# Two rows of indirect sends regrouped into four, in an attention loop followed by a mixture of experts

## The chip, the cores and the metric

The kernel runs on one core of a Trainium2 chip. The metric is the device time of one execution in microseconds (us). Engines: PE is TensorE (PEld its weight loads), DVE is VectorE, ACT is ScalarE, POOL is GpSimd, SP is SyncE.

## The reference

One transformer block over 32 batches of 256 rows of 256 numbers: a two-way cross attention (8 heads of 64) and a layer of 16 experts, of which each row takes its best four.

```python
def _L0_xattn_ref(x, context, Wq1, ..., Wout, bout):
    # q1,k1,v1 from x; q2,k2,v2 from context; 8 heads of 64
    attn1 = jax.nn.softmax(einsum('bhid,bhjd->bhij', q2, k1) * SCALE, axis=-1)
    out1  = einsum('bhij,bhjd->bhid', attn1, v1)
    attn2 = jax.nn.softmax(einsum('bhid,bhjd->bhij', q1, k2) * SCALE, axis=-1)
    out2  = einsum('bhij,bhjd->bhid', attn2, v2)
    out = out1 * alpha + out2 * (1.0 - alpha)
    ...
    return out @ Wout + bout

def _L0_ffn_ref(hidden_states, gate_w, w1, w3, w2):
    probs = jax.nn.softmax(x @ gate_w.T, axis=-1)
    topk_w, topk_idx = jax.lax.top_k(probs, 4)
    topk_w = topk_w / jnp.sum(topk_w, axis=-1, keepdims=True)
    ...
    act = silu(x @ w1[e]) * (x @ w3[e])
    out = sum over the four experts of topk_w * (act @ w2[e])

x = x + _L0_xattn_ref(_layernorm(x), ctx_1024, ...)
x = x + _L0_ffn_ref(_layernorm(x), ...)
```

## The kernel before

The program is written by hand: every engine has its own list of instructions, and the engines meet in semaphores. It has two long stages. In the attention loop `stage_a` calls an engine's `iteration(b, nxt, cur, prev, old)` once for each batch b; b = 2 to 30 is a real loop on the chip, and b = -1, 0, 1, 31, 32 and 33 stand before and behind it. The work of a batch spreads over several iterations: `nxt` starts batch b+1, `cur` is most of batch b, `prev` ends the attention of batch b-1, and `old` ends the routing of batch b-2. After the loop `stage_b` runs 80 groups of 256 rows through the experts, and a last part adds the results up.

The attention of a batch has eight steps, u = 0 to 7, each for two heads. For a step PE computes the scores into the PSUM tile `p_s`, DVE takes the negative row maxima (`nmx`, line 856), ACT takes the exponential (`probs`, line 619), DVE the reciprocal of the sums (`inv`, line 863, semaphore `inv_set`), and POOL multiplies in four instructions of one half head each (`normalise`, line 521, semaphore `normed_p`). PE transposes each head's 256 columns (`probs_half`, line 1150, semaphore `pt_done`), once it sees `normed_p` for that head: two of the four instructions for head 0, four for head 1. ACT copies head 0's half out of the PSUM tile `p_pt` (`probsT`, line 607, semaphore `pt_out_a`), DVE head 1's (line 760, `pt_out_b`), and PE multiplies with the values (`attend`, line 1170). The step of interest is the last one, u = 7 of batch b-1, which is worked off in iteration b. Behind its transposes PE stands before `project(b, 9)`, a query projection that writes into the bank of `p_pt` that ACT's copy reads, and so waits for `pt_out_a` of step 7.

POOL also sends. `send(i)` (line 513) is an indirect DMA that scatters 128 rows of 260 numbers from the tile `routed` to the rows of `x_rows` in HBM that `slot_i` names: a batch has eight of them (two halves of its rows, four experts each). The sends of batch b-2 stand in iteration b, behind two waits: for the slots from DVE (`router_step`, line 848) and for ACT's copies of the rows (`copies_set`, line 708). `rows_sent` counts them. DVE waits for it in the same iteration, before it writes `routed` for batch b-1 (`norm_apply`, line 778), which in turn needs POOL's reciprocal root `rstd` (`rsqrt`, line 508). That chain begins with `x_mid` (DVE, line 922), the output projection plus `x_res`; POOL writes `x_res` for the next batch (line 541) once `x_mid` has been read.

The order on POOL is the order in which the code is written; nothing reorders it.

Of the kernel before, what the change touches and what calls it, by code (L numbers as in the profile page):

```python
# [16 lines left out]
TOP_K = 4  # L17
# [4 lines left out]
def wait_alone(eng, sem, count):  # L22

    eng.wait_ge(sem, count)
    eng.nop(nofuse=True)
# [8 lines left out]
def spread(ap, axis, shape):  # L34

    return ap.unsqueeze(axis).to_broadcast(shape)


def wait(eng, sem, count):

    if isinstance(count, int) and count <= 0:
        return
    eng.wait_ge(sem, count)


def xattn_moe_kernel(nc, x, ctx, Wq1, Wk1, Wv1, Wq2, Wk2, Wv2, alpha_attn, Wout, bout,
# [8 lines left out]
    ST = S // P  # L55
    PAIRS = INNER // P
    STEPS = 2 * PAIRS
# [27 lines left out]
    with ExitStack() as stack:  # L85
# [218 lines left out]
        def norm1(b):  # L304

            return 1 if isinstance(b, int) and b == 0 else 2 * b

        def norm2(b, cur):

            return 2 * b + 1 if cur else 2 * b  # L310
# [33 lines left out]
        def stage_a(eng, body):  # L344
            body(-1, True, False, False, False)
            body(0, True, True, False, False)
            body(1, True, True, True, False)
            with eng.Fori(2, B - 1) as b:
                body(b, True, True, True, True)
            body(B - 1, False, True, True, True)  # L350
            body(B, False, False, True, True)
            body(B + 1, False, False, False, True)
# [3 lines left out]
        def stage_b(eng, body, before=0, after=3):  # L356

            for j in range(-before, LOADS):
                body(j, j % LOADS)
            with eng.Fori(1, GROUPS // LOADS - 1) as q:  # L360
                for r in range(LOADS):
                    body(LOADS * q + r, r)
            for j in range(GROUPS - LOADS, GROUPS + after):
                body(j, j % LOADS)

        def exists(j):

            return not isinstance(j, int) or 0 <= j < GROUPS
# [112 lines left out]
        @block.gpsimd  # L481
        def _(pool):
            for t in (ident, before, ones, routed):
                v = t[tuple([slice(None)] * len(t.shape))]
                pool.memset(v, 1.0 if t is ones or t is before else 0.0).then_inc(consts_set, 1)
            pool.wait_ge(consts_set, 4)
            pool.affine_select(out=ident[:, :], in_=ident[:, :], compare_op=ALU.not_equal, fill=1.0,
                               base=0, pattern=[[-1, P]], channel_multiplier=1).then_inc(consts_set, 1)

            pool.affine_select(out=before[:, :], in_=before[:, :], compare_op=ALU.is_gt, fill=0.0,  # L490
                               base=0, pattern=[[1, P]], channel_multiplier=-1).then_inc(consts_set, 1)
            pool.iota(pad_target[:, :, :], [[GROUP, 2 * E], [P, 2]], base=DUMP, channel_multiplier=1).then_inc(consts_set, 1)
            pool.memset(mhalf[:, :], -0.5).then_inc(consts_set, 1)
            for t, pattern, start, mult in (
                    (expert[:, :], [[1, E]], 0, 0),
                    (region[:, :], [[REGION, E]], 0, 0),
                    (base[:, :], [[REGION, E]], 0, 0),
                    (target[:, :, :], [[P * TOP_K, ST], [1, TOP_K]], 0, TOP_K),
                    (fills[:, :], [[GROUP, MOST]], 0, 0),
                    (tri[:, :, :], [[1, E], [-1, E]], 0, 0),  # L500
                    (group_no[:, :], [[P, TC]], 0, 1)):
                pool.iota(t, pattern, base=start, channel_multiplier=mult,
                          allow_small_or_imprecise_dtypes=True).then_inc(consts_set, 1)
            pool.wait_ge(const_in, 16 * N_CONST)

            def rsqrt(n):
                pool.wait_ge(ve_set, n)
                pool.tensor_tensor(rstd[:, :], ve[:, :], mhalf[:, :], ALU.pow).then_inc(rstd_set, 1)

            def send(i):  # L510

                t, k = i // TOP_K, i % TOP_K
                pool.indirect_dma_start(x_rows, bass.IndirectOffsetOnAxis(ap=slot_i[:, t, k:k + 1], axis=0),  # L513
                                        routed[:, t, k, :], None).then_inc(rows_sent, 16)

            def normalise(b, u):
                pool.wait_ge(inv_set, STEPS * b + u + 1)
                pr, rc = probs[u % 2], inv[u % 2]
                for h, t in ((0, 0), (0, 1), (1, 0), (1, 1)):
                    g = 2 * h + t  # L520
                    pool.tensor_tensor(pr[:, h, t, :], pr[:, h, t, :], rc[:, g:g + 1].to_broadcast([P, S]),  # L521
                                       ALU.mult).then_inc(normed_p, 1)

            def iteration(b, nxt, cur, prev, old):
                if prev:
                    normalise(b - 1, STEPS - 1)
                if old:
                    wait_alone(pool, router_step, ROUTER_STEPS * (b - 1))
                    wait_alone(pool, copies_set, b - 1)
                    for i in range(6):  # L530
                        send(i)
                if cur:
                    normalise(b, 0)
                    normalise(b, 1)
                if old:
                    for i in range(6, ST * TOP_K):
                        send(i)
                if cur:
                    wait(pool, mid_set, b)
                    pool.wait_ge(x_landed, 16 * (b + 1))  # L540
                    pool.tensor_tensor(x_res[:, :, :], x_in[:, :, :], spread(bias[:, :], 1, [P, ST, D]),
                                       ALU.add).then_inc(x_res_set, 1)
                if prev:
                    rsqrt(norm2(b, cur))
                if cur:
                    normalise(b, 2)
                    normalise(b, 3)
                if nxt:
                    rsqrt(norm1(b + 1))
                if cur:  # L550
                    for u in range(4, STEPS - 1):
                        normalise(b, u)

            stage_a(pool, iteration)

            def return_group(j, r):

                if exists(j):
                    wait_alone(pool, y_set, j + 1)
                    for i in range(2):  # L560
                        pool.indirect_dma_start(  # L561
                            y_rows, bass.IndirectOffsetOnAxis(ap=xg[r][:, i, D:D + 1].bitcast(I32), axis=0),
                            y_out[r % 4][:, i, :], None).then_inc(y_sent[r % 4], 16)

            stage_b(pool, return_group, after=0)
# [832 lines left out]
```

## Time and profile before

| | us |
|---|---|
| median of 3 runs | 2364.32 |
| lowest and highest of them | 2360.82 and 2365.71 |
| the profiled execution | 2342.8 |
| its span | 2341.0 |
| PE busy in the span | 1951.1 (83%) |
| POOL busy in the span | 1215.2 (52%) |

The attention loop takes the first two thirds of the span. In it a batch's period is the time from one batch's first send to the next batch's. The page's chain of work that ended last walks back from the last instruction to whatever released each step; "another core or an unknown queue" there, and "remote" in an engine's rows, stand for a release by something that the profile doesn't name. A row of the timeline gives start, duration, engine, line, operation, output and inputs, and in brackets the engine's idle time before it with what ended that.

### The profile page before, as it was taken

How to read it: one execution, taken by the hardware profiler on the slowest of the kernel's cores; microseconds unless marked ns; L12 is line 12 of the kernel's file. 1: busy time of each engine (PE TensorE's matmuls, PEld its weight loads, DVE VectorE, ACT ScalarE, POOL GpSimd, SP SyncE). 2: the span in 40 equal slices, each digit the busy share in tenths (PEclk: the TensorE clock that was granted, in tenths of full speed). 3: DMA queues.
4: the chain of work that ended last, by engine and by line, in shares of the span. 5: the costliest groups of instructions: out<-in, count | busy, mean ns of one | idle time of the engine just before them, and what ended most of it. 6: DMA issues, size and time to landing. Idle time of an engine off the chain costs nothing.

```text
span 2341.0 us, 52570 instructions
## 1 busy us (share of the span) xinstructions
PE 1951.1 (83%) x15778; PEld 1681.2 (72%) x15779; DVE 1423.4 (61%) x3205; ACT 1240.9 (53%) x3605; POOL 1215.2 (52%) x1683
## 2 busy tenths in 40 slices
PE   5799989999999998999999999995488888888700
PEld 4688877888777887788877878784377777777600
DVE  3466666666666676666666666665454444444488
ACT  4666656666566665666656666663144444444400
POOL 2356556656556565665655655564254545455500
PEclk9999999999999999999999999997699999999955
DMA  3511011110101101111011110114775444444399
GB/s 115 151 45 37 32 45 36 41 36 32 44 33 45 36 32 45 36 41 36 32 43 34 45 36 32 36 39 131 168 206 171 141 137 137 139 137 143 120 390 365
DMA packets 158599, 210.56 MB, mean 90 GB/s; under 512 B 24273, under 2 KB 131425, under 8 KB 158562
## 3 DMA queue, kind: packets, MB, share of 16 engines
q1 hardware_dynamic: 119394, 127.75, 18.2%
q0 software_dynamic: 26112, 71.86, 8.7%
q10 hardware_dynamic: 13056, 10.50, 1.6%
q8 instruction: 18, 0.29, 0.1%
q14 instruction: 19, 0.16, 0.0%
HBM read 113.02 MB, written 97.03 MB: 90 GB/s over the span
## 4 chain that ended last, share of the span: by engine, by line
PE 68%; another core or an unknown queue 11%; DVE 7%; ACT 4%; DMA 4%; issue 3%; SPq 2%; POOL 2%; ACTq 0%; POOLq 0%; DVEq 0%
PE p_av L1170 10%; PE p_pt L1150 9%; PE p_s L1074 7%; PE p_gu L1345 6%; PE p_s L1133 6%; PE p_y L1363 4%; PE p_x L1074 4%; PE p_s L1084 3%; DVE z_ahead L1044 3%; PE p_x L1203 3%; PE p_pt L1074 2%; PE p_xt L1334 2%; PE p_av L1074 2%; PE p_av L1084 2%
## 5 line engine op out<-in xcount | busy, mean ns | idle before, releaser
L521 POOL TENSOR_TENSOR probs<-probs,inv 128x256 f32<-128x256 f32 x1024 | 596.3, 615 | 496.0 <-DVE inv L863 495.9
L619 ACT ACTIVATE probs<-p_s,nmx 128x256 f32<-128x256 f32 x1024 | 474.0, 484 | 58.9 <-PE p_pt L1150 42.7
L856 DVE TENSOR_REDUCE nmx<-p_s 128x4 f32<-128x1024 f32 x256 | 312.4, 1221 | 254.2 <-PE p_s L1133 206.5
L561 POOL DMA_INDIRECT y_rows<-y_out,xg x288 | 276.3, 959 | 301.3 <-ACT y_out L731 231.1
L513 POOL DMA_INDIRECT x_rows<-routed,slot_i x256 | 253.8, 991 | 138.9 <-DVE target L848 69.1
L1150 PE MATMUL p_pt<-ident,probs 128*128 128x128 f32 x2048 | 293.8, 279 | 7.7 <-POOL probs L521 3.7
L607 ACT COPY probsT<-p_pt 128x512 f32<-128x512 f32 x256 | 151.4, 592 | 277.6 <-remote 152.7
L1170 PE MATMUL p_av<-probsT,val 128*64 128x256 f32 x2048 | 269.1, 408 | 2.0 <-ACT val L591 1.6
L1150 PEld LDWEIGHTS p_pt<-ident,probs 128*128 128x128 f32 x2048 | 227.7, 141 | 48.0 <-issue 17.8
L619 ACT ACTIVATION_READ_ACCUMULATOR probs<-p_s,nmx 128x1 f32 x1024 | 219.9, 215 | 0.0
L1170 PEld LDWEIGHTS p_av<-probsT,val 128*64 128x64 f32 x2048 | 144.3, 146 | 83.9 <-issue 28.0
L760 DVE COPY probsT<-p_pt 128x512 f32<-128x512 f32 x256 | 175.9, 687 | 45.3 <-PE p_pt L1150 33.6
L1015 DVE SCALAR_TENSOR_TENSOR gated<-gated,p_gu 128x256 f32<-128x256 f32 x144 | 60.0, 417 | 214.7 <-ACT gated L721 203.4
L1345 PE MATMUL p_gu<-wgu_hi,xgT_hi 128*128 x576 | 178.8, 310 | 11.4 <-issue 9.2
L721 ACT ACTIVATE gated<-p_gu 128x256 f32<-128x256 f32 x144 | 57.8, 402 | 239.9 <-PE p_gu L1345 139.3
L1133 PE MATMUL p_s<-kT_hi,qT_hi 64*128 64x256 f32 x1024 | 158.8, 306 | 9.6 <-ACT probs L619 7.5
L1345 PE MATMUL p_gu<-wgu_hi,xgT_lo 128*128 x576 | 165.1, 287 | 0.0
L1345 PE MATMUL p_gu<-wgu_lo,xgT_hi 128*128 x576 | 164.4, 285 | 0.0
L1074 PE MATMUL p_s<-rowsT_hi,wp_hi 128*128 128x256 f32 x512 | 151.8, 296 | 0.0
L1030 DVE TENSOR_TENSOR xgT_lo<-p_xt,xgT_hi 128x512 fp32r<-128x512 f32 x144 | 99.6, 692 | 76.7 <-ACT xgT_hi L736 54.9
L1133 PE MATMUL p_s<-kT_lo,qT_hi 64*128 64x256 f32 x1024 | 145.1, 280 | 0.4 <-issue 0.4
L1133 PE MATMUL p_s<-kT_hi,qT_lo 64*128 64x256 f32 x1024 | 144.7, 279 | 0.0
(192 smaller groups left out, 5199.3 us busy)
## 6 DMA issues: line engine op xcount, KB each, us to landing
xg<-x_rows SPq DMA_DIRECT2D x144, 257.0 KB
y_in<-y_rows SPq DMA_DIRECT2D x32, 1024.0 KB, 8.3
rows<-in_ctx_dram SPq DMA_DIRECT2D x32, 256.0 KB, 2.7
x_in<-in_x_dram SPq DMA_DIRECT2D x32, 256.0 KB, 2.7
mid_rows<-x_mid SPq DMA_DIRECT2D x32, 256.0 KB
z_ahead<-mid_rows SPq DMA_DIRECT2D x24, 256.0 KB
out_dram<-z_ahead ACTq DMA_DIRECT2D x24, 256.0 KB, 8.5
y_rows<-y_out,xg POOLq DMA_INDIRECT x288
```

What stands on the lines that cost most here:

```text
L513: pool.indirect_dma_start(x_rows, bass.IndirectOffsetOnAxis(ap=slot_i[:, t, k:k + 1], axis=0), routed[:, t, k, :], None).then_inc(rows_sen ...
L521: pool.tensor_tensor(pr[:, h, t, :], pr[:, h, t, :], rc[:, g:g + 1].to_broadcast([P, S]), ALU.mult).then_inc(normed_p, 1)
L561: pool.indirect_dma_start(y_rows, bass.IndirectOffsetOnAxis(ap=xg[r][:, i, D:D + 1].bitcast(I32), axis=0), y_out[r % 4][:, i, :], None).th ...
L607: act.copy(flat(probsT[u % 2][:, 0, :, :]), p_pt[:, 0, :]).then_inc(pt_out_a, 1)
L619: act.activation(probs[u % 2][:, h, t, :], p_s[:, 2 * (u % 2) + h, t * S:(t + 1) * S], ACT.Exp, bias=nmx[u % 2][:, g:g + 1], accum_out=sum ...
L760: dve.tensor_copy(flat(probsT[u % 2][:, 1, :, :]), p_pt[:, 1, :]).then_inc(pt_out_b, 1)
L856: dve.tensor_reduce(nmx[i][:, :], p_s[:, 2 * i:2 * i + 2, :].rearrange("p h (t k) -> p (h t) k", t=ST), AX.X, ALU.max, negate=True).then_i ...
L1074: mm = pe.matmul(proj_bank(n)[:, j * S:(j + 1) * S], wp[a][:, w, k, c:c + P], rowsT[w // 3][r][:, k, :], start=(i == 0), stop=(i == 5))
L1133: mm = pe.matmul(p_s[:, 2 * d + h, t * S:(t + 1) * S], qT[d][q][r:r + HEAD_DIM, p, t * P:(t + 1) * P], kT[d][k][r:r + HEAD_DIM, p, :], sta ...
L1150: mm = pe.transpose(p_pt[:, h, k * S + t * P:k * S + (t + 1) * P], probs[u % 2][:, h, t, k * P:(k + 1) * P], ident[:, :])
L1170: mm = pe.matmul(p_av[r:r + HEAD_DIM, 0:S], val[d][:, k, c:c + HEAD_DIM], probsT[u % 2][:, h, k, :], start=(d == 0 and k == 0), stop=(d == ...
L1345: mm = pe.matmul(p_gu[:, i, n, :], xgT[i][h][:, n, k, :], wgu[a][:, bass.ds(experts[r], 1), k, :, :].rearrange("p e g i -> p (e g i)"), st ...
```

## The change

POOL's iteration alone is rewritten. A batch's eight sends stood in two rows, six and two. Now they stand in rows of two, three and two, and one by itself: the first two between the halves of `normalise(b - 1, 7)` (head 0 before them, head 1 behind), then three, then as before the normalisations of steps 0 and 1, then two, then `x_res`, then the last one, ahead of `rsqrt`.

```diff
-            def normalise(b, u):
+            def normalise(b, u, heads=(0, 1)):
                 pool.wait_ge(inv_set, STEPS * b + u + 1)
                 pr, rc = probs[u % 2], inv[u % 2]
-                for h, t in ((0, 0), (0, 1), (1, 0), (1, 1)):
+                for h, t in [(h, t) for h in heads for t in range(ST)]:
...
                 if prev:
-                    normalise(b - 1, STEPS - 1)
+                    normalise(b - 1, STEPS - 1, (0,))
                 if old:
                     wait_alone(pool, router_step, ROUTER_STEPS * (b - 1))
                     wait_alone(pool, copies_set, b - 1)
-                    for i in range(6):
+                    for i in range(2):
+                        send(i)
+                if prev:
+                    normalise(b - 1, STEPS - 1, (1,))
+                if old:
+                    for i in range(2, 5):
                         send(i)
                 if cur:
                     normalise(b, 0)
                     normalise(b, 1)
                 if old:
-                    for i in range(6, ST * TOP_K):
+                    for i in range(5, 7):
                         send(i)
                 if cur:
                     wait(pool, mid_set, b)
                     pool.wait_ge(x_landed, 16 * (b + 1))
                     pool.tensor_tensor(x_res[:, :, :], x_in[:, :, :], spread(bias[:, :], 1, [P, ST, D]),
                                        ALU.add).then_inc(x_res_set, 1)
+                if old:
+                    send(7)
                 if prev:
                     rsqrt(norm2(b, cur))
```

On POOL, at the head of the loop's body (b = 2 to 30), where step 7 of batch b-1 is normalised and the sends of batch b-2 begin; L521 is `normalise`, L513 a send:

```order
-L521 TENSOR_TENSOR probs<-probs,inv 128x256 x4
+L521 TENSOR_TENSOR probs<-probs,inv 128x256 x2
 L24 REGISTER_ALU
-L513 DMA x_rows<-routed,slot_i 139264x260 x6
+L513 DMA x_rows<-routed,slot_i 139264x260 x2
+L521 TENSOR_TENSOR probs<-probs,inv 128x256 x2
+L513 DMA x_rows<-routed,slot_i 139264x260 x3
 L517 ISA
```

Head 1 of step 7 has moved behind the wait for the slots and behind two sends, and the row of six is now two, a pause of two normalisations, and three.

On POOL, further down in the same body, behind the normalisations of steps 0 and 1; L541 (L546 in the changed kernel) is `x_res`, L508 `rsqrt`:

```order
 L513 DMA x_rows<-routed,slot_i 139264x260 x2
-L540 ISA
-L541 TENSOR_TENSOR x_res<-x_in,bias 128x512
+L545 ISA
+L546 TENSOR_TENSOR x_res<-x_in,bias 128x512
+L513 DMA x_rows<-routed,slot_i 139264x260
 L507 ISA
 L508 TENSOR_TENSOR rstd<-ve,mhalf 128x2
```

The last send now stands between `x_res` and the `rstd` for which DVE waits. The other engines' lists are the same in both kernels.

## Rows read from the trace of the kernel before

**Rows 1.** The page: the chain of work that ended last, share of the span by engine

```profile
PE 68%; another core or an unknown queue 11%; DVE 7%; ACT 4%; DMA 4%; issue 3%; SPq 2%; POOL 2%; ACTq 0%; POOLq 0%; DVEq 0%
```

**Rows 2.** Timeline of PE, one batch (columns: start us, us, instruction)

```profile
736.71 0.66 PE L1150 MATMUL p_pt<-ident,probs 128*128 128x128 f32 x4
...
738.65 0.65 PE L1150 MATMUL p_pt<-ident,probs 128*128 128x128 f32 x4
742.25 0.38 PE L1074 MATMUL p_pt<-rowsT_hi,wp_hi 128*128 128x256 f32 x1 [2.95 <-ACT probsT L607]
...
744.03 3.40 PE L1170 MATMUL p_av<-probsT,val 128*64 128x256 f32 x16
```

**Rows 3.** Timeline of ACT, the same batch

```profile
741.62 0.59 ACT L607 COPY probsT<-p_pt 128x512 f32<-128x512 f32 x1 [5.56 <-remote]
```

**Rows 4.** All copies of line 607 in the span: why ACT waited, who waited

```profile
  remote: 152.7, 28
...
  PE p_pt L1074: 77.2, 26
```

**Rows 5.** Timeline of POOL, the same batch

```profile
733.07 1.06 POOL L513 DMA_INDIRECT x_rows<-routed,slot_i  x1 [1.81 <-DVE target L848]
...
739.50 0.96 POOL L513 DMA_INDIRECT x_rows<-routed,slot_i  x1 [0.30 <-issue]
...
750.41 0.96 POOL L513 DMA_INDIRECT x_rows<-routed,slot_i  x1 [0.30 <-issue]
753.51 1.29 POOL L541 TENSOR_TENSOR x_res<-x_in,bias 128x512 f32<-128x512 f32 x1 [2.13 <-DVE x_mid L922]
754.90 0.72 POOL L508 TENSOR_TENSOR rstd<-ve,mhalf 128x2 f32<-128x2 f32 x1
755.61 4.71 POOL L521 TENSOR_TENSOR probs<-probs,inv 128x256 f32<-128x256 f32 x8
```

**Rows 6.** Windows: busy time of PE, PEld, DVE, ACT, POOL, then PE's clock, DMA

```profile
742.25:749.00 6.75, 6.75 (x53) 4.75 (x53) 1.21 (x4) 4.46 (x18) 4.61 (x8) 0.75 0.00 0
```

**Rows 7.** Timeline of POOL: first sends of five batches, and one pause

```profile
190.75 1.06 POOL L513 DMA_INDIRECT x_rows<-routed,slot_i  x1 [1.81 <-DVE target L848]
...
831.88 1.06 POOL L513 DMA_INDIRECT x_rows<-routed,slot_i  x1 [1.81 <-DVE target L848]
836.24 0.97 POOL L513 DMA_INDIRECT x_rows<-routed,slot_i  x1 [3.30 <-issue]
...
877.86 1.06 POOL L513 DMA_INDIRECT x_rows<-routed,slot_i  x1 [1.81 <-DVE target L848]
...
1516.32 1.06 POOL L513 DMA_INDIRECT x_rows<-routed,slot_i  x1 [1.81 <-DVE target L848]
```

**Rows 8.** Timeline of ACT and of PE in the batch that begins at 831.88

```profile
836.21 0.59 ACT L607 COPY probsT<-p_pt 128x512 f32<-128x512 f32 x1 [1.35 <-PE p_pt L1150]
...
843.51 0.37 ACT L611 COPY attnT<-p_av 128x256 f32<-128x256 f32 x1 [2.57 <-remote]
```

```profile
843.36 0.40 PE L1133 MATMUL p_s<-kT_lo,qT_hi 64*128 64x256 f32 x2 [0.43 <-issue]
```

**Rows 9.** Timeline of DVE, then of PE, behind the sends

```profile
755.73 1.25 DVE L778 TENSOR_SCALAR routed<-x_mid,mv,rstd 128x256 f32<-128x256 f32 x2 [0.91 <-POOL rstd L508]
756.91 0.68 DVE L760 COPY probsT<-p_pt 128x512 f32<-128x512 f32 x1
```

```profile
759.40 1.95 PE L1170 MATMUL p_av<-probsT,val 128*64 128x256 f32 x16
```

**Rows 10.** DMA from 748 to 754 us in 40 slices (tenths busy)

```profile
DMA  0000000000000000047910000099500000000000
```

**Rows 11.** Timelines behind the loop (b = 32): ACT, POOL's last send, DVE

```profile
1613.85 0.37 ACT L611 COPY attnT<-p_av 128x256 f32<-128x256 f32 x1 [3.11 <-PE p_av L1170]
```

```profile
1617.95 0.96 POOL L513 DMA_INDIRECT x_rows<-routed,slot_i  x1 [0.30 <-issue]
```

```profile
1622.42 0.73 DVE L778 TENSOR_SCALAR routed<-x_mid,mv,rstd 128x256 f32<-128x256 f32 x2 [3.54 <-DMA x_rows<-routed,slot_i]
```

## The prediction

> **What bounds the kernel now.** I read the chain of work first: PE carries 68% of it, and the second largest share, 11%, is put down to nothing that the profile names [rows 1]. So the attention loop is bound by PE except where something unnamed holds it. The timelines of one batch show where. PE transposes head 0 of step 7 at 736.71, which takes 0.66, so ACT's copy could start at about 737.4. It starts at 741.62, after 5.56 idle that "remote" ended [rows 2, 3]: 4.2 us late. PE, done with head 1 at 739.30, stands still for 2.95 until that copy is out. All its other work in the loop runs back to back. The stall also costs clock: of the 6.75 us behind it, PE was granted 0.75 on average, that is 1.2 instead of 2.4 GHz for half of it, and the 16 matmuls of `attend` at 744.03 take 3.40 [rows 2, 6]. The span has 28 such waits of ACT, and 26 of them made PE idle, 77.2 us in sum or 2.97 each [rows 4].
>
> What holds the copy? ACT waits there only for a semaphore that PE's transposes raise. While that rise is missing, POOL is in its row of six sends, 733.07 to 740.46 [rows 5]; the rise arrives some 1.1 us after the row's last send. The trace holds an experiment of its own on this. In the batch that begins at 831.88, POOL pauses 3.30 after its first send, for no reason that the profile shows, and sends one and five [rows 7]. There the copy waits 1.35, and PE's transposes end the wait as they should. The unnamed wait appears later instead, inside the second part of the row (2.57 before 843.51), and costs PE 0.43 [rows 8]. So I read: **from about the third send in an unbroken row, PE's signals reach the others late, until about 1.1 us after the row.** A broken row lets them through.
>
> **The terms.** From the first send at 190.75 to that at 1516.32 are 27 periods in 1325.57 us. The one with the pause takes 877.86 - 831.88 = 45.98 [rows 7]. The other 26 take (1325.57 - 45.98) / 26 = 49.22 each. The pause was worth 3.24 us a batch, and 26 batches give 26 x 3.24 = 84.2. That is the nearest row for the gain. The other end is a stall gone altogether: the pause batch still has 0.43 of PE idle there [rows 8]; 0.43 x 26 = 11.2 more, 95.4 in all. I take half of the 11.2, since a row of three should still delay a little: 89.8. The last batch of the loop's tail has one more such stall (two of the 28 waits lie outside the 26); I allow it 2.3 of the 2.97. Sum: 92.1.
>
> What the edits cost. **Head 1 of step 7 behind two sends.** The first two sends stay at 733.07 to about 735.4, since they wait for the same slots. Two normalisations of 0.59 (4.71 / 8) follow, done by about 736.7. PE wants head 1 at 738.65, so 1.9 us cover it [rows 2, 5]. It costs nothing; without the cover it would be 3 us or so a batch. **The row of three** then runs from about 736.8 to 740.3, no later than the row of six ended. Head 0's signal (737.4) falls into its first send, head 1's (about 739.2) just ahead of its third. If the latter is late until 741.4, ACT's next exponentials and DVE's copy for `attend` come about 1.5 late, which PE feels as half a microsecond, since it has `project(b, 9)` and one `attend` to do: this is what the 5.6 left out stands for. **Sends five and six** follow the normalisations of steps 0 and 1, as the old row of two did. **The last send** stands between `x_res` and `rstd`. It takes 0.96 plus 0.15 to 0.30 of gaps, so `rstd` comes 1.1 to 1.3 later against `x_mid`. DVE waits for its landing too. The old last send started at 750.41 and its bytes were moved by 752.35 [rows 5, 10], so I take 2.3 from start to landing. The new one starts about 1.45 after `x_res` does and so lands 3.75 after it, while DVE now starts `norm_apply` 755.73 - 753.51 = 2.22 after it: 1.5 late. Behind that, DVE's copy ends at 757.59 and PE's second `attend`, the second half of the 16 matmuls at 759.40, wants it at 760.3 [rows 9]. So 2.7 us of cover for 1.5: nothing, with 1.2 left. POOL's normalisation of step 2 has two of its four done by 756.8, 1.1 later by 757.9; PE transposes them just before the `attend` at 759.40, from about 758.8 [rows 5, 9]: nothing, with 0.9 left. Behind the loop (b = 32) the eight sends become two and six, with about the same end, and the landing of the last sets the pace there: nothing.
>
> What would be late next is PE itself. Its work fills the period to 45.55 (45.98 less the 0.43), and no other engine comes near: POOL is busy for half of the span.
>
> The Trainium skill, page SBUF — State Buffer, section "SBUF: two separate sides", says that PE, ACT and DVE's dedicated port pair never wait on anyone, and that DMA and compute can't slow each other. By it the sends hold nobody up, the order on POOL is free, and the change is worth nothing; that is the first rival below. The two batches with and without the pause differ by 3.24 us and disagree with it, as far as one batch can.
>
> **Rivals.** *The pause is too short.* The pause seen was 3.30; the new one is two normalisations and two gaps, about 1.4. If the hold-up counts sends through it, the five sends act as one row that ends at 740.3, ACT's copy still starts at about 741.6, and the time stays as it is: 2364. For it speaks that no pause as short is in the trace; against it, that the signals come through 1.1 us behind a row. A milder form is a row half drained: ACT's copy is held to 739 or 740, PE idles 1 to 1.5 instead of 2.97, and the clock sometimes falls. That gives half of the sum, 26 x 1.8 = 47: about 2317. *The sends are not the cause.* Behind the loop eight sends stood in one row, and ACT's wait in the midst of it, 3.11 before 1613.85, was ended by PE as usual [rows 11]. So a long row alone does not do it. If the cause is something that merely shared the pause's batch, the time stays too. PE had much less to do there, which may be the other half of the condition. *The last send holds DVE (the slower side).* DVE's write of `routed` waits for its landing. Behind the loop, with other transfers on the queues, a landing took 1622.42 - 1617.95 = 4.47 [rows 11], and here the store of `x_mid` and the load of `x_in` start in the same microseconds. It decides from 2.3 + 1.2 = 3.5 from start to landing; at 4.47 PE's `attend` is 1.0 late, 29 batches x 1.0 = 29. With the stall gone this only trims the gain to about 63 (2301); with the pause too short as well it ends at 2364 + 29 = 2393.
>
> **How the numbers follow.** The stall gone or nearly: 0.62, including the trimmed gain. Half drained: 0.19. No effect, by the short pause or another cause: 0.12, of which a little falls to either side of 0.2%. Slower by the last send: 0.07. On the profiled execution, 2342.8 - 92.1 = 2250.7. The median of the runs is 21.5 above that execution; I have no row that says where, so I take the same 92.1 off it: 2364.3 - 92.1 = 2272.2. Low end: a stall gone altogether in all 29 batches, 95.4 + 3 x 3.67 = 106.4, and 6 more in case part of those 21.5 are such stalls: 2252. High end: it must hold half drained with its uncertainty, and leave out only the unchanged and the slower: 2325. A measurement of this kernel tells about 0.2% (4.7 us) from no change. Faster by more than that: 0.62 + 0.19 + 0.02 = 0.83; within it 0.09; slower 0.08.
>
> **What would show it.** Right: the period falls to 45.5 to 46.0; ACT's copy of step 7 starts within a microsecond of its transposes, with PE as the releaser; the 2.95 before `project(b, 9)` is gone and the clock there is 1.00; "another core or an unknown queue" loses its part in the loop but keeps what it has among the experts. The row of three shows at most a short unnamed wait on DVE's copy or ACT's exponentials. The last send: DVE's wait before line 778 grows from 0.91 to about 2.4, put down to the sends, and PE doesn't notice. Wrong: the unnamed wait is still there, ending about 1.1 behind the third send of the row of three; or PE idles before the second `attend` of step 1 for DVE's copy.

## The result, and the profile after

| | before | after |
|---|---|---|
| median, us | 2365.02 (4 runs, 2360.82 to 2369.14) | 2231.27 (4 runs, 2228.13 to 2232.74) |
| ratio | | 0.9433 [0.9413, 0.9452] |
| the profiled execution | 2342.8 | 2231.67 |
| mean period, 27 batches of the loop | 49.10 | 44.80 |
| first to last send of the experts' stage | 538.4 | 548.1 |

The change saves 133.8 us. The forecast had the direction and the mechanism, and missed the size: it said 92.1 and a range of 2252 to 2325, and the time lies 21 us below the range.

The page's chain of work that ended last, which answers to [rows 1]:

```profile
PE 73%; DVE 7%; ACT 5%; another core or an unknown queue 4%; DMA 4%; issue 3%; SPq 2%; POOL 1%; ACTq 0%; POOLq 0%; DVEq 0%
```

The unnamed share fell from 11% to 4%. By itself that share shows little: the row of five below also stands at 4%, though its copy of step 7 is held, because the profile names PE as the releaser there. The starts of the copies have to be read too. All copies of ACT at what was line 607 and is now line 614, which answers to [rows 4] (columns: why ACT waited, us and times):

```profile
L614 ACT COPY probsT<-p_pt x256: 577/591/608, 45.3 to 1488.7; 128x512 f32<-128x512 f32 x128
its engine sat idle before it (us, times) until:
  PE p_pt L1157: 167.9, 125
  issue: 0.3, 1
```

No wait is "remote" any more. The same head of the loop's body as in [rows 2, 3, 5], by the timelines of POOL, then ACT, PE and DVE (columns as there):

```profile
727.00 1.06 POOL L513 DMA_INDIRECT x_rows<-routed,slot_i  x1 [2.49 <-DVE target L855]
728.37 0.96 POOL L513 DMA_INDIRECT x_rows<-routed,slot_i  x1 [0.30 <-issue]
729.35 1.20 POOL L521 TENSOR_TENSOR probs<-probs,inv 128x256 f32<-128x256 f32 x2
730.71 1.01 POOL L513 DMA_INDIRECT x_rows<-routed,slot_i  x1 [0.17 <-issue]
...
733.29 0.96 POOL L513 DMA_INDIRECT x_rows<-routed,slot_i  x1 [0.30 <-issue]
```

```profile
732.08 0.59 ACT L614 COPY probsT<-p_pt 128x512 f32<-128x512 f32 x1 [1.63 <-PE p_pt L1157]
...
735.08 0.47 ACT L626 ACTIVATE probs<-p_s,nmx 128x256 f32<-128x256 f32 x1 [0.58 <-remote]
```

```profile
731.11 0.66 PE L1157 MATMUL p_pt<-ident,probs 128*128 128x128 f32 x4
...
732.90 0.60 PE L1157 MATMUL p_pt<-ident,probs 128*128 128x128 f32 x4
733.25 0.36 PE L1081 MATMUL p_pt<-rowsT_hi,wp_hi 128*128 128x256 f32 x1
...
734.86 2.15 PE L1177 MATMUL p_av<-probsT,val 128*64 128x256 f32 x16
```

```profile
735.08 0.69 DVE L767 COPY probsT<-p_pt 128x512 f32<-128x512 f32 x1 [1.53 <-remote]
```

ACT's copy starts 0.3 behind the end of head 0's transposes (731.77), in the midst of POOL's row of three. PE goes from head 1 straight into the projection; the 2.95 us are gone. What the forecast said of the row of three is there too: head 1's transposes end at 733.50, inside the third send, and ACT's next exponentials and DVE's copy both start at 735.08, 1.6 later, with nothing named as the releaser. PE feels it as 0.2 of `attend` (2.15, where 1.95 is usual).

Two windows in answer to [rows 6], the place of the old stall and then the whole period (columns: us; PE, PEld, DVE, ACT, POOL busy; PE's clock; DMA share and GB/s):

```profile
733.25:737.00 3.75, 3.75 (x31) 2.53 (x29) 1.08 (x3) 3.17 (x15) 2.02 (x3) 1.00 0.20 71
727.00:771.80 44.80, 44.73 (x387) 38.42 (x386) 31.14 (x74) 30.66 (x94) 29.25 (x43) 1.00 0.12 41
```

PE is busy for 44.73 of the period's 44.80 and is granted the full 2.4 GHz throughout, so the loop is bound by PE's own work here, give or take the 0.2.

The last send, by the timelines of POOL and DVE (in answer to [rows 5, 9]):

```profile
743.21 1.29 POOL L546 TENSOR_TENSOR x_res<-x_in,bias 128x512 f32<-128x512 f32 x1 [0.22 <-issue]
744.66 0.99 POOL L513 DMA_INDIRECT x_rows<-routed,slot_i  x1 [0.16 <-issue]
```

```profile
747.78 1.11 DVE L785 TENSOR_SCALAR routed<-x_mid,mv,rstd 128x256 f32<-128x256 f32 x2 [3.26 <-DMA x_rows<-routed,slot_i]
```

DVE's wait grew from 0.91 to 3.26, since the send takes 3.12 until its landing releases DVE (744.66 to 747.78), and PE does not notice.

### The profile page after: what moved, and what is told of

Its sections match the earlier page's. It is cut to its first block, busy times and chain, and to the rows that moved or that the text cites. A ratio compares the mean times of both kernels' runs of the same rounds, so it can differ in the third digit from the quotient of the medians.

```text
span 2229.9 us, 52570 instructions
## 1 busy us (share of the span) xinstructions
PE 1912.0 (86%) x15778; PEld 1658.6 (74%) x15779; DVE 1391.4 (62%) x3205; ACT 1240.7 (56%) x3605; POOL 1220.2 (55%) x1683
## 4 chain that ended last, share of the span: by engine, by line
PE 73%; DVE 7%; ACT 5%; another core or an unknown queue 4%; DMA 4%; issue 3%; SPq 2%; POOL 1%; ACTq 0%; POOLq 0%; DVEq 0%
PE p_pt L1157 11%; PE p_s L1140 9%; PE p_av L1177 9%; PE p_s L1081 8%; PE p_gu L1352 7%; PE p_y L1370 5%; PE p_x L1081 4%; PE p_s L1091 4%; PE p_x L1210 3%; DVE z_ahead L1051 3%; ACT probs L626 3%; PE p_xt L1341 2%; PE p_av L1081 2%; PE p_at L1362 2%
## 5 line engine op out<-in xcount | busy, mean ns | idle before, releaser
L521 POOL TENSOR_TENSOR probs<-probs,inv 128x256 f32<-128x256 f32 x1024 | 598.3, 615 | 398.0 <-DVE inv L870 397.0
L513 POOL DMA_INDIRECT x_rows<-routed,slot_i x256 | 256.4, 1002 | 150.8 <-DVE target L855 90.6
L1177 PE MATMUL p_av<-probsT,val 128*64 128x256 f32 x2048 | 256.9, 390 | 2.9 <-ACT val L598 2.7
L1177 PEld LDWEIGHTS p_av<-probsT,val 128*64 128x64 f32 x2048 | 136.7, 138 | 79.2 <-issue 20.8
```

What stands on the lines that cost most here:

```text
L1177: mm = pe.matmul(p_av[r:r + HEAD_DIM, 0:S], val[d][:, k, c:c + HEAD_DIM], probsT[u % 2][:, h, k, :], start=(d == 0 and k == 0), stop=(d == ...
```

## The experiments

The theory: a long unbroken row of sends on POOL delays the signals that PE raises, and a pause in the row lets them through. Rivals: the gain comes from moving work on POOL (less in the first row, a later last send); the row must only be shorter, pause or not; the cause is the traffic that the sends make, not their issue; the change does nothing and something outside made the difference.

**A condition without the hold-up.** In the first set of runs the kernel before itself took 2092.66 (31 runs, 2088.49 to 2096.41), not 2365. Four variants ran there, all edits of the changed kernel, and in none of their four traces is there an unnamed release. The changed kernel itself did not run in that set. Two take the pause away or replace it (the filler's tile and its first fill are left out of the cut):

```diff
 (row of five: step 7 whole, then five sends)
-                    normalise(b - 1, STEPS - 1, (0,))
+                    normalise(b - 1, STEPS - 1)
...
-                    for i in range(2):
-                        send(i)
-                if prev:
-                    normalise(b - 1, STEPS - 1, (1,))
-                if old:
-                    for i in range(2, 5):
+                    for i in range(5):
                         send(i)
```

```diff
 (filler pause: step 7 whole, two sends, idle work, three sends)
+            def pause():
+                for n in range(2):
+                    pool.tensor_tensor(filler[:, n, :], filler[:, n, :], mhalf[:, 0:1].to_broadcast([P, 256]), ALU.mult)
...
-                    normalise(b - 1, STEPS - 1, (0,))
+                    normalise(b - 1, STEPS - 1)
...
-                if prev:
-                    normalise(b - 1, STEPS - 1, (1,))
-                if old:
+                    pause()
```

The short pause is the filler pause with one idle multiplication of two columns; "two, four, two" is the changed kernel with four sends behind the pause and two further down.

> The changed kernel without its pause: step 7 is normalised whole, then five sends stand in one row; the 2 and the 1 stay. If an unbroken row holds PE's signals from its third send on (row theory), ACT's copy of step 7 is held until about 1.1 us after the fifth send, one send (1.3 us) sooner than before: PE idles about 1.7 instead of 2.95 a batch and the clock dips less often, so 2300 to 2340. If what counted were the number of sends ahead of steps 0 and 1 (six to five) or the last send's new place, it keeps the changed kernel's time, about 2231.

> Step 7 is normalised whole ahead of the sends, and between the second and the third send POOL does two idle multiplications of the same size on a tile that nobody reads. Row theory: the pause alone does it, 2226 to 2240, as the changed kernel. If it is the later release of head 1 (PE's order of work) that helps, the time is near that of a row of five, 2300 or more.

> As the run with the filler pause, but the pause is one multiplication of two numbers a row, some 0.3 us with its gaps. If the hold-up has to drain for about 1.1 us after a send, such a pause is too short and the time is near that of a row of five (2300 to 2340). If any other instruction between two sends resets it, 2225 to 2240.

> The changed kernel with four sends behind the pause instead of three, and two before x_res. Row theory: the third and fourth of four hold PE's signals about 1.3 us longer than a row of three does (head 1's signal, project(b, 9), the first attend), and PE feels 0.3 to 0.8 a batch more: 2240 to 2256. If two sends and a pause are all that matters, 2231; the last send's old place can't cost more than that.

Measured against the kernel before beside them: row of five 0.9990 [0.9978, 1.0002], filler pause 1.0010 [0.9999, 1.0020], short pause 0.9993 [0.9982, 1.0004], two-four-two 1.0005 [0.9995, 1.0016]. All four are the same as before, and all four periods are 44.5. The chain on the page of the row of five, and its timelines of POOL (the last of its five sends) and of ACT:

```profile
PE 81%; DVE 6%; DMA 5%; issue 3%; POOL 2%; SPq 2%; ACT 1%; POOLq 0%; DVEq 0%; ACTq 0%
```

```profile
726.24 1.06 POOL L513 DMA_INDIRECT x_rows<-routed,slot_i  x1 [1.81 <-DVE target L850]
...
731.40 0.96 POOL L513 DMA_INDIRECT x_rows<-routed,slot_i  x1 [0.30 <-issue]
```

```profile
730.58 0.59 ACT L609 COPY probsT<-p_pt 128x512 f32<-128x512 f32 x1 [1.35 <-PE p_pt L1152]
```

"Another core or an unknown queue" is not in the chain at all, and ACT copies on time in the midst of five sends. So a long row does not hold PE's signals by itself; it needs a condition that was absent here. Where it is absent, these orders on POOL cost nothing against each other. From the second trace of before (below) to this row of five, the loop up to the first send of b = 32 is 142.8 shorter and the experts' stage 131.7, so I take nearly all of 2365 less 2093 as hold-up. Every expectation of these four that named a difference missed for this reason, and they tell nothing of pauses. All four ran again in the other condition.

**The kernel before once more**, unchanged, to see which condition holds and to have a second trace of it.

> The kernel before, unchanged, profiled again. The runs of before that stood beside the last four kernels took 2092.66, 272 less than the first ones, and in the profiles of those four kernels no signal of PE is held, neither in the loop nor among the experts. If the hold-up comes with the chip or its condition and not with the program, this profile shows either the row of six with ACT's copy on time, periods of 44.5 and a time near 2093, or, in the first condition, the 5.5 us waits again and 2343 to 2366. If the hold-up depends on something drawn anew at each load, it may lie between.

It took 2364.11, and the kernel before beside it 2369.99, one run each: the hold-up was back. The record gives this set and the set at 2093 the same chip number, 160 seconds apart, so the chip's number doesn't tell the two conditions apart. All its copies of line 607:

```profile
L607 ACT COPY probsT<-p_pt x256: 579/591/609, 42.4 to 1625.0; 128x512 f32<-128x512 f32 x128
its engine sat idle before it (us, times) until:
  remote: 153.9, 27
```

The waits are those of [rows 4]. But the copies span 1582.6 us here and 1566.1 in the first trace of the same kernel:

```profile
L607 ACT COPY probsT<-p_pt x256: 579/591/609, 44.1 to 1610.2; 128x512 f32<-128x512 f32 x128
```

These 16.5 more stand against the 21.5 us for which the forecast had no row. The experts' stage is 8.7 longer too (547.1 here, 538.4 there), and the rest of the program somewhat shorter. Of the 27 periods from the second on, the first trace had five near 48.1 and one of 50.7 among those near 49.4; this one has one of 48.2 and three near 50.9.

**How long must the pause be?** The same edits where the hold-up acts (the kernel before beside them: 2361.14, 2357.36 to 2365.89), and a fourth with one idle multiplication of 256 columns (beside a kernel before of 2365.63, 2361.41 to 2368.51).

> The same kernel as in the run e2_row_of_five (step 7 whole, then five sends in one row, then two, and one), to be read beside a kernel before of about 2365, where the hold-up is there. Row theory: ACT's copy of step 7 is held until about 1.1 us after the fifth send, PE idles about 1.7 a batch, 2300 to 2340. Number-of-sends theory: 2231. Should before stand at 2093 again, the condition decides and this is 2090.

> The kernel of e5_short_pause again (one tiny multiplication as the pause), beside a before of about 2365. If the hold-up has to drain for about 1.1 us, 2300 to 2340; if any instruction between two sends resets it, 2225 to 2240.

> As e4b (step 7 whole, two sends, idle pause, three sends), but the pause is one multiplication of 0.6 us instead of two, some 0.9 us between the second send's end and the third's start; e5b had some 0.3 to 0.4, e4b 1.4. Where before stands near 2365: if the hold-up must drain for about 1.1 us it is still there, 2290 to 2312, as a row of five (2312); if 0.9 is enough, 2227. If before stands at 2093, nothing is told apart.

> The kernel of e4_filler_pause again (two idle multiplications between the second and third send, step 7 whole ahead), beside a before of about 2365. Row theory: the pause alone does it, 2226 to 2240. Order-of-head-1 theory: 2300 or more.

| | gap behind the second send | us | ratio | period |
|---|---|---|---|---|
| row of five | 0.31 | 2311.72 | 0.9783 [0.9767, 0.9800] | 46.9 or 48.2 |
| short pause | 0.39 | 2310.29 | 0.9781 [0.9760, 0.9801] | 46.8 or 48.2 |
| one filler | 0.82 | 2232.73 | 0.9438 [0.9423, 0.9454] | 44.75 |
| two fillers | 1.39 | 2226.84 | 0.9428 [0.9410, 0.9445] | 44.53 |

The gap runs from the end of one send to the start of the next. Timelines of the row of five: its last send, ACT's copy and PE's projection.

```profile
723.08 0.96 POOL L513 DMA_INDIRECT x_rows<-routed,slot_i  x1 [0.30 <-issue]
```

```profile
725.20 0.59 ACT L609 COPY probsT<-p_pt 128x512 f32<-128x512 f32 x1 [4.31 <-PE p_pt L1152]
```

```profile
725.84 0.39 PE L1076 MATMUL p_pt<-rowsT_hi,wp_hi 128*128 128x256 f32 x1 [1.63 <-ACT probsT L609]
```

The copy starts 1.16 behind the last send's end (724.04), as before (1.16 behind 740.46); with one send less it comes 1.26 sooner and PE idles 1.63 instead of 2.95. That is somewhat over a third of the gain, from one send less in the row (the last send's new place is in this run too, and is tried below). (The profile names PE here, not "remote"; head 0's transposes were done at 722.2, 3.0 before, so the wait is the same.) The short pause and the filler pause, POOL and ACT each:

```profile
718.30 0.20 POOL L520 TENSOR_TENSOR filler<-filler,mhalf 128x2 f32<-128x2 f32 x1
718.67 0.99 POOL L515 DMA_INDIRECT x_rows<-routed,slot_i  x1 [0.16 <-issue]
...
721.22 0.96 POOL L515 DMA_INDIRECT x_rows<-routed,slot_i  x1 [0.30 <-issue]
```

```profile
723.26 0.58 ACT L618 COPY probsT<-p_pt 128x512 f32<-128x512 f32 x1 [4.32 <-PE p_pt L1161]
```

```profile
726.67 1.19 POOL L520 TENSOR_TENSOR filler<-filler,mhalf 128x256 f32<-128x256 f32 x2
728.03 1.01 POOL L515 DMA_INDIRECT x_rows<-routed,slot_i  x1 [0.17 <-issue]
```

```profile
728.66 0.59 ACT L618 COPY probsT<-p_pt 128x512 f32<-128x512 f32 x1 [1.34 <-PE p_pt L1161]
```

A gap of 0.39 does nothing: the five sends act as one row, and the copy is held to 1.08 behind the last. A gap of 1.39 frees it fully, and this kernel differs from the row of five by the pause alone: step 7 stands whole ahead of the sends in both. So it is the pause, and that the pause is filled with useful normalisations does not matter. The point from which a gap suffices lies between 0.39 and 0.82, lower than the 1.1 that I had read from the signals' arrival behind a row.

**The issue, or the traffic?** Three more sends behind the row of three, each with one number of a row (4 bytes) where a real one carries 260:

```diff
+            def narrow(i):
+                t, k = i // TOP_K, i % TOP_K
+                pool.indirect_dma_start(spare_rows, bass.IndirectOffsetOnAxis(ap=slot_i[:, t, k:k + 1], axis=0),
+                                        routed[:, t, k, 0:1], None).then_inc(rows_sent, 16)
...
                     for i in range(2, 5):
                         send(i)
+                    for i in range(3):
+                        narrow(i)
```

> The changed kernel with three more indirect sends behind the row of three, which makes a row of six there; they scatter one number a row (4 bytes) instead of 260. The order and number of descriptors are as for the full ones, the bytes next to none. If it is POOL's making of descriptors, send after send, that holds PE's signals, ACT's and DVE's unnamed waits behind steps 7 come back at full size (ACT's exponentials and copies held until 1.1 us after the sixth), 2290 to 2370. If it is the moved data, a hold-up as after the row of three, 2232 to 2250, the rest being POOL's longer row.

2340.09, 0.9893 [0.9876, 0.9909] of the kernel before beside it (2365.63), so four fifths of the gain are lost again. Timelines of POOL (the last narrow send), ACT and PE:

```profile
732.78 0.96 POOL L520 DMA_INDIRECT spare_rows<-routed,slot_i  x1 [0.31 <-issue]
```

```profile
735.13 0.59 ACT L612 CAST qT_hi<-p_pt 128x512 fp32r<-128x512 f32 x1 [3.22 <-remote]
```

```profile
732.89 0.29 PE L1149 MATMUL p_s<-kT_hi,qT_hi 64*128 64x256 f32 x2
733.62 0.38 PE L1149 MATMUL p_s<-kT_lo,qT_hi 64*128 64x256 f32 x1 [0.44 <-issue]
734.35 0.37 PE L1149 MATMUL p_s<-kT_lo,qT_hi 64*128 64x256 f32 x1 [0.35 <-issue]
735.08 0.45 PE L1149 MATMUL p_s<-kT_hi,qT_lo 64*128 64x256 f32 x2 [0.36 <-issue]
```

A send of 4 bytes a row takes POOL the same 0.96 us and holds the others like a full one. The hold-up meets other signals than before: ACT's copy of step 7 is on time, and its next copy (`qT_hi`) waits 3.22, until 1.39 behind the last narrow send (733.74). So the bytes moved are not what counts. Whether it is the issue on POOL or the 128 small writes that each send still makes, this run does not tell. Not all of the 109 us has to be hold-up, for the three sends also keep POOL busy for 3.8 us a batch, but the traces put little of it on POOL. The 27 periods take 1296.5 where after takes 1209.5, 87.0 more. In them PE waits 31.0 for nothing that the profile names ("issue"; 0.2 in after), 8.4 for POOL's normalisations (0.5) and 2.8 for DVE, and counts 44.8 more as busy. 11.5 of the rest lie behind the loop. PE's rows show a second thing. These matmuls are one group of `scores` that wait for nothing and raise one signal at the end, and normally start 0.12 apart. From 732.89 to 735.08 they start 0.73 apart. So PE itself crawls once the row is long enough, not only its signals are late.

**Where the sends stand.** Two-four-two again, and with the last send back ahead of `x_res` (rows of two, three and three); then the kernel before with three sends ahead of steps 0 and 1 and five behind, so a row of three without any pause.

```diff
 (two-four-two)
-                    for i in range(2, 5):
+                    for i in range(2, 6):
...
-                    for i in range(5, 7):
+                    for i in range(6, 8):
...
-                if old:
-                    send(7)
```

```diff
 (last send back)
-                    for i in range(5, 7):
+                    for i in range(5, 8):
...
-                if old:
-                    send(7)
```

```diff
 (three and five, against the kernel before)
-                    for i in range(6):
+                    for i in range(3):
...
-                    for i in range(6, ST * TOP_K):
+                    for i in range(3, ST * TOP_K):
```

> The kernel of e1_two_four_two again (four sends behind the pause, two before x_res), beside a before of about 2365. Row theory: 0.3 to 0.8 a batch more than the changed kernel, 2240 to 2256; if only the first two sends and the pause matter, 2231.

Two-four-two: 2232.16, 0.9452 [0.9436, 0.9468], the same as the change. I had expected the fourth send to cost. Timelines of POOL (the last of the four sends behind the pause), ACT and DVE:

```profile
734.33 0.96 POOL L513 DMA_INDIRECT x_rows<-routed,slot_i  x1 [0.30 <-issue]
```

```profile
734.85 0.47 ACT L624 ACTIVATE probs<-p_s,nmx 128x256 f32<-128x256 f32 x1 [0.58 <-remote]
```

```profile
734.85 0.69 DVE L765 COPY probsT<-p_pt 128x512 f32<-128x512 f32 x1 [1.52 <-remote]
```

Head 1's signals come through at 734.85, in the midst of the fourth send and 0.83 behind the third's end (734.02). In the changed kernel it is 0.83 behind the third's end too (735.08 against 734.25), with no fourth. So "late until 1.1 behind the row" does not hold as a rule for every row: it fits the rows of five and six, where the signal was raised during the fourth send, and not this one, where it was raised during the third.

> The changed kernel with its last send back beside the two before x_res (rows of two, three, three). My terms put the last send's place at nothing. If the third send of that second row of three holds PE's signals (value projections, ACT's copies) while PE has slack there, 2229 to 2236; if DVE's wait for the last landing (3.3 us in the changed kernel) was costing something, 2215 to 2226; if the lone place was what kept a second hold-up away, 2240 to 2265.

> The kernel before with three sends in the first row and five in the second (behind steps 0 and 1), no pause, nothing else moved. Row theory: the third of three still holds head 0's signal until about 1.1 us after it, 0.0 to 1.0 late instead of 4.2, so the stall before project(b, 9) is mostly gone; but the row of five stands where PE makes its output projection and the values, and holds their signals from its third send on: ACT's value copies and x_mid up to 3 us late, 2240 to 2300. If a row of five hurts only at the first place, 2232 or less.

These two ran in a condition between the others: the kernel before took 2337.57 beside them (2315.81 to 2344.22), so the ratios alone can be compared. Last send back: 2202.30, 0.9428 [0.9369, 0.9487], the same as the change's 0.9433. So the new place of the last send makes no difference that can be told, but the interval is 14 us wide to either side, and the hold-up was weaker in this trace: DVE's copy of head 1 waits about 0.7 instead of 1.5, and the period is 44.5. Two-four-two, which has no lone last send either and ran under the full hold-up, stands at 0.9452. Three and five: 2250.23, 0.9617 [0.9547, 0.9687]. A row of three leaves ACT's copy alone (its wait was 1.46, ended by PE's transposes), but five sends behind the normalisations put `x_res` late on POOL, and the chain on the page shows where the time went:

```profile
PE 41%; POOL 19%; issue 14%; DVE 11%; another core or an unknown queue 6%; DMA 4%; ACT 2%; SPq 2%; POOLq 0%; DVEq 0%; ACTq 0%
```

So in this set a shorter first row was enough to be rid of the stall; it was not tried under the full hold-up. The pause is what allows five sends before the normalisations, and so keeps POOL off the critical path.

**The same remedy among the experts.** There ACT still waits for something unnamed in the changed kernel (79.6 us at line 728 by the view that groups by line). The stage has 144 groups (the trace has 288 sends, two a group), not the 80 named where the kernel is described. POOL sends each group's rows in pairs, two pairs often in one row. The experiment puts one idle multiplication of 256 columns behind each pair (its tile and first fill are left out of the cut):

```diff
+                    pool.wait_ge(filler_set, j + 1)
+                    pool.tensor_tensor(filler[:, r, :], filler[:, r, :], mhalf[:, 0:1].to_broadcast([P, 256]), ALU.mult).then_inc(filler_set, 1)
```

> The changed kernel, with one idle multiplication of 0.6 us behind each group's two sends in the expert stage, where POOL's sends stand in rows of four (two groups) and PE's signals are held from the third one on. The stage takes 547 us here, 416 in the runs without any hold-up. If 0.9 us between two rows of two lets the signals through, a group costs what POOL needs, 3.4 us instead of 3.8 for most groups: 2190 to 2215. If 0.9 is too short, the rows only get longer: 2232 to 2290.

2182.88, 0.9234 [0.9216, 0.9251]: the fastest version under the full hold-up, 2.1% below the changed kernel by the two ratios and 7 us below the range expected, with work that computes nothing. The loop takes the same as in the changed kernel (1341.6 against 1341.2 from first send to that of b = 32). First and last send of the experts' stage in the changed kernel and in this one, and the two groups of ACT by line (columns: busy, mean ns, idle before and what ended it):

```profile
L568 POOL DMA_INDIRECT y_rows<-y_out,xg x288: 955/961/972, 1563.8 to 2111.9; - x144
```

```profile
L573 POOL DMA_INDIRECT y_rows<-y_out,xg x288: 956/968/1012, 1563.6 to 2059.8; - x144
```

```profile
L728 ACT ACTIVATE gated<-p_gu 128x256 f32<-128x256 f32 x144 | 58.0, 403 | 256.1 <-PE p_gu L1352 153.1 <-remote 79.6 <-PE p_at L1362 21.3
```

```profile
L735 ACT ACTIVATE gated<-p_gu 128x256 f32<-128x256 f32 x144 | 56.2, 390 | 164.4 <-PE p_gu L1359 93.1 <-remote 51.6 <-PE p_at L1369 12.2
```

The stage falls from 548.1 to 496.2. In the condition without the hold-up it takes 415.4 (1557.8 to 1973.2 in the row of five), so 81 us more are held there, and unnamed waits are left. Which row of sends holds them I did not try.

## Why the prediction was wrong in its size

**What held the copy** was read rightly. It was the row of sends; a pause of two normalisations frees head 0's signal; the trace of after shows each step that the forecast named: period down (to 44.8, below the 45.5 to 46.0 that it gave), PE as the releaser of ACT's copy, the clock at 1.00, a short unnamed wait from the row of three. The row of five and the filler pause share the gain out: one send less in the row brings 2.2% (0.9783), the pause the rest (0.9428), and neither needs the half heads. What in the chip holds PE's signals, and when, stays open.

**The period was one term mis-sized.** The sum took the one batch with a natural pause, 45.98, as what a freed batch takes, plus half of its 0.43 of PE's idle time: 3.24 and 0.22 a batch, 89.8 for 26. Measured on the same 27 periods, after takes 1209.5 where before took 1325.6, that is 116.1, and 26.3 more than the 89.8. Its 26 batches without a natural pause take 44.76 each, so a batch gains 4.46 and not 3.45. The pause batch was not a free one: it took 1.2 more than a freed batch, not 0.43. The row that I had quoted, 843.36 with 0.43 idle [rows 8], was the visible end of it. The row ahead of it in the same timeline of PE in the kernel before is the rest:

```profile
842.33 0.61 PE L1133 MATMUL p_s<-kT_hi,qT_hi 64*128 64x256 f32 x2
843.36 0.40 PE L1133 MATMUL p_s<-kT_lo,qT_hi 64*128 64x256 f32 x2 [0.43 <-issue]
```

Such rows start 0.12 apart as a rule; these two stand 1.03 apart, so 0.91 is lost, of which only 0.43 counts as idle and the rest as a busy matmul. It looks like the crawl that the narrow sends show at length. Another 0.20 is PE's wait for POOL's late normalisation at 844.66, which is the natural pause's own doing: after has that pause too, in one batch of 45.78, with 0.54 of such a wait. I took PE's idle time as its loss, and called 45.55 the floor where it is 44.5 (filler pause) to 44.8.

**The edges of the loop** were a second, smaller one: I allowed 2.3 for the last batch's tail, and the three periods at both ends of the 27 together fell by 6.9, 4.6 more. Both together make the sum 30.9 too small for the loop (123.0 against 92.1).

**The step from the profiled execution to the runs** was the other large miss. The forecast took 92.1 off the runs as off the profiled execution, so it put the 21.5 between them at nothing in the sum, for want of a row. Against the profiled execution the gain is 2342.8 - 2231.67 = 111.1 (123.0 in the loop, less 9.8 that the experts' stage was short in that first trace, less 2.1 elsewhere). Against the runs it is 133.8. The second trace of before is 15.9 longer in the loop, with the same kind of waits. So I read the difference as hold-up that the first execution happened to have less of, where the change takes it away; that rests on two traces. Against the second one the loop gains 138.9. So of the 41.7 missing, 22.6 are this, and 19.0 are the sum's own (30.9 in the loop, less the 9.8 and the 2.1). The low end allowed 6 for it and should have allowed all 21.5; at 2236 it would still have been 5 too high, for the period.

**The costs called nothing** were nothing. Head 1 of step 7 behind two sends has no price: PE takes it at 732.90, as soon as it gets there. The last send behind `x_res` costs nothing that can be told: the run with it put back stands at 0.9428 against 0.9433, under a weaker hold-up, and in after PE has no wait behind it. It did not go quite by the working: it takes 3.12 to land, not 2.3, and DVE's wait came to 3.26, not 2.4. It stayed under the 3.5 from which I had it decide. The row of three costs 0.27 a batch (44.80 against 44.53 for the filler pause, where DVE copies head 1 at 730.39, before the third send of the row starts; that this is the cause is read from the rows, not tried); the forecast had half of 0.43. The clock's part also went as read: PE at 1.00 from 727.00 to 771.80.

**The rivals.** The pause too short: no, and it is not near, since a gap of 0.82 does nearly as well. Half drained: no. The last send holding DVE: no. That the sends are not the cause, and the order on POOL is free: true of the condition in which the row of five copies after 1.35 and four orders agree with before within 0.1%; not where the hold-up acts, and there sends of 4 bytes a row from POOL go with PE's own matmuls starting 0.73 apart instead of 0.12. The Trainium skill, page SBUF — State Buffer, section "SBUF: two separate sides", says that PE never waits on anyone, and that DMA and compute can't slow each other; it says so of the ports of SBUF. Where the forecast read it as "sends hold nobody up", the measurement decides against that reading. Whether the ports have a part in it, no run here shows. The caution that a long row behind the loop went unpunished [rows 11] was sound: a row alone is not enough. What the other part of it is was not found.

## What to carry to other kernels

When a wait is ended by something that the profile can't name, look at what POOL is issuing just then; if it is a row of indirect DMAs, put other work, useful or idle, between them. In this kernel it was enough to have 0.8 us from one send's end to the next one's start, behind the second send. A wait can also be ended by an engine that the profile names but that was done long before; that is the same case. When a trace holds a natural experiment, size it by the distance between the starts of instructions and by the period, not by the idle time beside them: an engine that crawls counts as busy. And where the runs lie above the profiled execution, take a second trace of the same kernel before saying what a change is worth on the runs.

## What the runs showed of the hardware

- The same program, the kernel before, took 2093, 2338 and 2365 us in different sets of runs, each steady within itself to between 0.4 and 1.2%. The traces put the difference on PE's signals during rows of indirect sends, in the loop (period 44.5 for the row of five in the first set, 49.5 for the second trace of before) and among the experts (415 against 547). What switches it is open.
- With the hold-up, an order on POOL alone is worth 5.7%, and idle work on POOL among the experts about 2.1% more. Without it, four orders of the loop take the time of the kernel before within 0.1%.
- A gap of 0.39 us between sends does nothing, 0.82 does nearly all, and 1.39 all. With 4 bytes a row instead of 1040 an indirect send still takes 0.96 us on POOL, and the others are still held.
- PE's own matmuls can be slowed in a long row of sends: in the run with narrow sends they start 0.73 apart, where 0.12 is usual, and about half of that time counts as busy.
- When a held signal comes through depends on when it was raised: about 1.1 behind the last send for one raised during the fourth of five or six, 0.83 behind the third for one raised during the third, whether a fourth follows or not. No model of mine covers both.
